# Two multi-head attentions: where the matmuls of the last maxima, the turning of the maxima and the last weighted sums stand in TensorE's order

## What is computed

```
def mha(xq, ctx, wq, wk, wv, wo, bo):
    q = (xq @ wq) ...; k = (ctx @ wk) ...; v = (ctx @ wv) ...      # 16 heads of 64
    scores = jnp.einsum('bhqd,bhkd->bhqk', q, k) / math.sqrt(DH)
    attn = jax.nn.softmax(scores, axis=-1)
    out = jnp.einsum('bhqk,bhkd->bhqd', attn, v)
    return out.transpose(0, 2, 1, 3).reshape(b, sq, INNER) @ wo + bo
h1 = adaln(x, t, norm1_w, norm1_b)
x = mha(h1, h1, ...) + x
h2 = adaln(x, t, norm2_w, norm2_b)
x = mha(h2, context, ...) + x
```

## Time and profile before

| | us |
|---|---|
| median of 3 runs | 4986.73 |
| lowest and highest | 4986.18, 4992.08 |
| the profiled execution | 4994.57 |
| its span (first to last instruction) | 4992.7 |
| first attention, from its first projection to its last multiplication | 4190.8 to 4522.0 |
| second attention, likewise | 4557.8 to 4769.9 |

### The profile page before, as it was taken

How to read it: one execution, slowest core, us unless ns; L and a number is a source line. 1 busy time by engine, 2 the same in 40 slices (tenths; PEclk the granted TensorE clock), 3 DMA queues, 4 the chain that set the end, 5 groups by cost and what they waited for, 6 DMA issues and landing times. The chain is left out here.

```text
span 4992.7 us, 88759 instructions
## 1 busy us (share of the span) xinstructions
PE 4213.4 (84%) x25255; PEld 2688.7 (54%) x25606; DVE 3516.2 (70%) x17560; ACT 2256.3 (45%) x7321; POOL 377.2 (8%) x306
## 2 busy tenths in 40 slices
PE   8999999999999998578888888888733696997879
PEld 6888888888888886423333333333322453333346
DVE  7888888888888886566777777777544594443335
ACT  4555555555555554245555555555522121331213
POOL 0000000000000000111111111111001001331000
PEclk9999999999999998788888888888865697996569
DMA  0000000000000000122222222222000010000001
GB/s 28 2 2 2 2 2 2 2 2 2 2 2 2 2 2 22 39 57 58 49 53 48 53 50 46 50 46 47 16 5 3 15 35 25 12 8 16 15 5 34
DMA packets 82327, 106.84 MB, mean 21 GB/s; under 512 B 26096, under 2 KB 75435, under 8 KB 79916
## 3 DMA queue, kind: packets, MB, share of 16 engines
q1 hardware_dynamic: 81899, 101.85, 8.5%
HBM read 70.74 MB, written 30.26 MB: 20 GB/s over the span
## 5 line engine op out<-in xcount | busy, mean ns | idle before, releaser
L287 DVE CUSTOM_DVE_ANT_0 I-219junk<-I-215encw,I-218expo,I-227rec 128x77 f32<-128x77 f32 x3072 | 941.7, 357 | 6.3
L1315 DVE TENSOR_REDUCE I-41383nmax<-ps 128x1 f32<-128x512 f32 x768 | 501.4, 685 | 218.0 <-PE ps L984 211.4
L1203 ACT ACTIVATE I-41386prob<-ps 128x512 f32<-128x512 f32 x768 | 428.4, 596 | 227.5 <-PE ps L1021 145.3
L265 ACT ACTIVATE I-217tanh_s<-ps 128x77 f32<-128x77 f32 x1024 | 242.2, 237 | 594.2 <-PE ps L245 594.2
L245 PE MATMUL ps<-I-212hist,I-49small 128*128 128x77 f32 x2048 | 456.4, 304 | 41.1 <-DVE I-212hist L323 40.8
L245 PEld LDWEIGHTS ps<-I-212hist,I-49small 128*128 128x128 f32 x2048 | 305.1, 188 | 297.4 <-DVE I-212hist L323 297.2
L251 PE MATMUL ps<-I-217tanh_s,I-49small 128*128 128x77 f32 x2048 | 454.6, 304 | 0.0
L984 PE MATMUL ps<-I-41377kS,I-41376qS 96*128 96x512 bf16 x768 | 332.1, 458 | 128.5 <-DVE I-41383nmax L1315 58.1
L247 PE MATMUL ps<-I-212hist,I-216uh_h 128*128 128x128 f32 x2048 | 439.8, 296 | 0.0
L252 PE MATMUL ps<-I-212hist,I-49small 128*128 128x128 f32 x2048 | 439.8, 296 | 0.0
L273 ACT ACTIVATE I-223hh<-I-229gate_t,I-228pre,I-222rh 128x1 f32<-128x1 f32 x1024 | 395.5, 386 | 84.6
(11 more groups left out here) (508 smaller groups left out, 7568.5 us busy)
## 6 DMA issues: line engine op xcount, KB each, us to landing
I-41376qS<-parts SPq DMA_DIRECT2D x24, 768.0 KB, 7.7
parts<-I-41395room SPq DMA_DIRECT2D x36, 384.0 KB, 2.5
parts<-I-41395room SPq DMA_DIRECT2D x36, 256.0 KB, 2.3
I-41377kS<-parts SPq DMA_DIRECT2D x12, 768.0 KB, 8.1
parts<-I-41395room SPq DMA_DIRECT2D x36, 128.0 KB, 1.8
I-49small<-in_layers SPq DMA_DIRECT2D x6, 768.0 KB, 9.0
I-41376qS<-I-41385mrow SPq DMA_DIRECT2D x192, 2.0 KB
I-41376qS<-I-41392crow SPq DMA_DIRECT2D x192, 2.0 KB
```

Of the source, the lines that this page charges most:

```text
L287: return e.tensor_tensor_reduce(junk[:, 2 * g + b, :], encw[:, g, b, :], expo[:, b, :], inv[:, b:b + 1], rec[:, b, g:g + 1], ALU.mult, ALU ...
L1203: e.activation(prob[:, tau % 2, j, :], k.ps[:, b, :], ACT.Exp, scale=scale).then_inc(free[b], 1)
L1315: e.tensor_reduce(nmax[:, U % HG, i, j:j + 1], k.ps[:, use[0], :], AX.X, ALU.max, negate=True).then_inc(free[use[0]], 1)
```

## The change

In the first attention `max_scores` of the last query tile goes ahead of the scores of the last key tile: max(3), scores(3), weigh(2). In both attentions `turn_max` goes ahead of the last `weigh`. The first attention then ends a unit with max(3), scores(3), weigh(2), turn, weigh(3); the second with scores(0), sums, values, max(0), turn, weigh(0). There `nk - 1` is 0, so that the first edit changes nothing. No instruction is added or taken away, no wait of another engine is changed, and the preparation ahead of unit 0 stays.

```
--- before
+++ after
@@ in TensorE's pair() of attention3
                         at = k0 - keys[b][0][0]
+                        if following and x_ and x_ == nk - 1:
+                            max_scores(G + 1, 1 - u, x_)
                         if not (first(G) and x_ == 0):
                             e.wait_ge(s.prob, G * (2 * nk) + 2 * x_)
...
                             if x_ == 0:
                                 e.wait_ge(s.qkept, G * 2 + 4)
-                            max_scores(G + 1, 1 - u, x_)
-                    weigh(nk - 1)
+                            if x_ == 0 or x_ < nk - 1:
+                                max_scores(G + 1, 1 - u, x_)
                     if following:
                         turn_max(G + 1)
+                    weigh(nk - 1)
```

## The result

| | us |
|---|---|
| before, median of 11 runs | 4987.61 (4984.88 to 4995.18) |
| after, median of 11 runs | 5002.23 (4995.76 to 5008.19) |
| ratio | 1.0026, 95% interval 1.0017 to 1.0036 |
| span of the profiled execution after | 5005.8 |

The kernel became slower by 0.26%, some 13 us with an interval from 8.5 to 18; the two medians lie 14.6 apart. The median, 5002.23, is 6.7 above the forecast of 4995.5 and inside the range of 4990 to 5003, by 0.8 us. The estimate passes the bound of 0.2%, on the side to which 0.48 had been given, but the interval reaches down to 0.17%.

What follows compares the result with a forecast made beforehand. TensorE, busy 84% of the span, was taken as the bound, with VectorE's chain releasing the second attention's turning. 16.8 - 4.5 - 3.5 = 8.8 us more on 4986.73 gave 4995.5 us, range 4990 to 5003.

Steps and rivals of the forecast that it cites:

- the side to which 0.48 had been given: Whole program: slower by more than about 0.2%, 10 us; chance 0.48, against 0.46 for same and 0.06 for faster.
- First attention: Unit's end: 0.18 us saved by the order, 0.12 by casts ahead of GpSimd's sum; 4.5 us less over 15 units.
- Second attention, the order: weigh(0) goes between turning and projection, lengthening every unit's loop by 1.12 us; 16.8 us more over 15 units.
- Second attention, the clock: Rises to full clock number 5 or 6 instead of 3, each worth 1.45 us or more; 3.5 us less.
- The sum: Whole program: 16.8 - 4.5 - 3.5 = 8.8 us more, 4995.5 us, 0.18% more.
- the clock that does not help: Second attention: rises stay near 3; +12.3 to +14 us, 4999 to 5001; chance 0.20, shared with less first-attention gain.
- a smaller gain in the first attention: First attention saves less than forecast, program +12 to +18 us; chance 0.20, shared with the clock not helping.
- it would help so much as to make the change a gain: Second attention: clock rises in most units, program 4977 us; chance 0.06 for faster by over 10 us.
- the clock falls in the first attention: First attention: 1.33 us of gathered idle time lowers the clock; once a unit 51 us, 5050; chance 0.04.
- weigh(3) waits: First attention: exponentials 0.2 late use up the 0.19 margin; gain 2 instead of 4.5 us, 4998; no separate chance.

Runs made afterwards that it cites:

- the single ones: Against before, first attention only: turning ahead of weigh(3) with max(3) left, 5004.43 us, ratio 1.0027; max(3) moved with turning left, 4999.89 us, ratio 1.0015.
- the filled versions: Before and after, each with idle matmuls on zeros in every second-attention unit, ten and fourteen: 4954.38 us, ratio 0.9919, and 4951.62 us, ratio 0.9917, to before.
- the early split: Before and after, each with VectorE splitting maxima ahead of normalising in the second attention: 4980.35 us, ratio 0.9980, and 4992.04 us, ratio 1.0005, to before.
- the control: The kernel before built anew with no change, against before: ratio 1.0000 (0.9991 to 1.0009).
- the version with the second move alone: Against before, only the turning put ahead of weigh(0) in the second attention, first attention unchanged: 5009.82 us, ratio 1.0041.
- the version with the turning alone: Against before, first attention only: turning put ahead of weigh(3), max(3) left in its old place: 5004.43 us, ratio 1.0027.
- split_first: Against before, VectorE splits the next pair's maxima ahead of normalising in the second attention: 4980.35 us, ratio 0.9980.
- before_filled: Against before, ten idle matmuls on zeros in each second-attention unit, behind weigh(0) and ahead of the turning: 4954.38 us, ratio 0.9919.

## Why the prediction was right

*First attention.* The steps came as worked out: 1.33 us of idle time ahead of max(3), none ahead of the turning or the projection, the casts free of GpSimd. 18.94 us a unit was forecast and 18.94 was measured; 4.5 us in all, and 4.54. That the two edits act together was not said in the prediction, and is what the single ones showed. The rule of the Trainium skill on the shared port pair ("SBUF — State Buffer", section "Who interferes with whom") agrees with the traces: the casts took 0.304 us at the median with GpSimd's sum beside them, and 0.174 without it.

*Second attention, the order.* VectorE's 4.94 us stayed, weigh(0) went between the turning and the projection, and the distance grew from 1.32 to 2.43, where 2.42 was forecast. An ordinary unit is 14.24 us and was forecast at 14.2. That the size hangs on the low clock is shown by the filled versions, and that VectorE's order releases the turning by the early split.

*Second attention, the clock.* The direction was right and the picture was not. I expected 5 or 6 rises of the same length as before. There were seven over the 14 units, six of them for 3.4 us and not 6.8 (two are the last rows of the first view above, at 0.99). The idle time in which such a unit ends is longer now, 3.57 us in the timeline above against 2.65 in the earlier trace rows, which may be why; no run isolates it. A unit with a rise was 12.88 to 13.43 us. Against 14.24 for each of the 14 the rises gave back 14 x 14.24 - 192.15 = 7.2 us; before it was 14 x 13.11 - 179.1 = 4.4. That is 1.03 us for each of seven rises, where 1.45 or more had been put for each of 5 or 6. So the term is -2.8 and was forecast at -3.5: more rises, each worth less, two errors that nearly cancel.

*The sum.* The terms came to 4.54 less and 12.52 + 1.16 more, +9.1 us against a forecast of +8.8. The ratio's 13 us is more. The interval of the change reaches down to 8.5, so this difference may be chance: where the clock rises and falls elsewhere moves a profile by several us, as the control and the first copies show. It is harder to say so of the version with the second move alone: its terms come to 12.7 (11.6 over its 15 units and the last weigh(0)), and its interval starts at 13.5. Whether something beyond the two stages pays a few us for the move stays open; no run settled it. With 13 or 14.6 us the measured time lies where the prediction had put the clock that does not help or a smaller gain in the first attention, +12 to +18, with a chance of 0.20, and neither came true. That it stayed within the range, whose upper end is +17 (5003.7 when added up, not 5003), is in part luck.

*The rivals.* That the clock would not help: it did, by 2.8 us. That it would help so much as to make the change a gain: not by itself, but with the clock held up the move's cost falls to 0.24 us a unit. That the clock falls in the first attention: not in the 84 such units of the six profiles with both edits, where the idle time is 1.33 us; in the version with the turning alone, with up to 1.97 us, it fell six times. With before's order it is not free of falls either: of the five profiles that have it, three had one (the control, `split_first` and `before_filled`), always in the same unit, which took 20.96 us and not 19.3. So the trace before, which had none, showed the stage at its best. The Trainium skill's warning ("TensorE: Matmul & The Clock Gate", section "A second HAM failure mode: psum-queue depth-cycling") did not hold for the change. It fits the version with the turning alone, whose clock swung six times with a pause in every unit, though no run shows whether the cause that the page names is the one here. That weigh(3) waits: it did not in the change; with the turning left behind it, it waited 0.16 us, where 0.2 was expected.

## What to carry to other kernels

When work is put behind an instruction that waits, ask what stands behind it in turn: weigh(3) covered a copy and cost nothing once max(3) had been made early, weigh(0) left an idle place and went into the chain that releases the next unit, and both moves are the same edit in one line of shared code. Read which chain releases the wait, and whether the moved work lies in the loop behind it, for each stage that calls the code. And look at the clock of the stage: where TensorE is at half clock because it idles in a loop of VectorE's, filling the idle time was worth 37 us here, more than any order tried.

## What the runs showed of the hardware that was not expected

The granted clock of one kernel varies by execution in where it falls: the control, the same program as before, had one fall of 3.4 us in the first attention, the trace before had none. With before's order of that stage it fell in 3 of 70 units, behind idle times of 0.97 and 0.69 us round a turning, such as stand in many units without a fall. A single idle time of 1.97 us ahead of the turning was followed by such a fall in 6 of 8 units, one of 1.75 or 1.76 in none of 6, one of 1.33 ahead of the maxima in none of 84. And with ten matmuls on zeros in each unit of the second attention, 2.33 us of 9.75, the clock stayed at 1.00 for 143 us, where it had been at 0.56 on average; the time of the whole program fell by 0.8%.
